# Attention's last two heads: one exponential in place of two for three packs, with rounding and two remainders on VectorE

## What is computed

```
scores = jnp.einsum('bqhd,bkhd->bhqk', q, k) / np.sqrt(HD).astype(np.float32)
mask = jnp.tril(jnp.ones((l, l), dtype=bool))
scores = jnp.where(mask, scores, jnp.float32(-1e+30))
p = jax.nn.softmax(scores, axis=-1)
o = jnp.einsum('bhqk,bkhd->bqhd', p, v)
```

## Time and profile before

| | us |
|---|---|
| median of three runs | 2253.05 (2245.42 to 2260.81) |
| the profiled execution, its time | 2254.39 |
| the profiled execution, its span | 2252.3 |
| attention's remainders on GpSimd, first to last start | 346.1 to 686.4 |
| drain, from the last head's row maxima to the next stage's first matmul | 663 to 690.8 |

### The profile page before, as it was taken

The page is one execution under the profiler, slowest core; times in us unless marked ns, Lnnn a source line. Parts: engine busy times, 40 slices in busy tenths (PEclk is TensorE's granted clock), DMA queues, the critical chain, the costliest instruction groups (busy, mean ns, idle before and its releaser), DMA issues.

```text
span 2252.3 us, 34615 instructions
## 1 busy us (share of the span) xinstructions
PE 2123.3 (94%) x11176; PEld 1724.2 (77%) x11176; DVE 1452.6 (64%) x1950; ACT 1087.4 (48%) x1700; POOL 1180.6 (52%) x717
## 2 busy tenths in 40 slices
PE   6898989999997999799999999999889999999999
PEld 4777766666666888688888899999667877877877
DVE  6787766777765888445655537776856565756563
ACT  3444447888884877622222336666523232223231
POOL 0111137999997887400000068777667376665463
PEclk8999988999998999899999999999999999999999
DMA  5678763333324765377898657878988699797795
GB/s 187 206 237 259 249 184 86 96 105 98 99 68 135 274 228 215 131 237 260 302 324 272 217 195 281 303 299 303 323 292 279 219 321 327 252 298 253 253 320 194
DMA packets 259627, 516.92 MB, mean 230 GB/s; under 512 B 20978, under 2 KB 136690, under 8 KB 240964
## 3 DMA queue, kind: packets, MB, share of 16 engines
q1 hardware_dynamic: 259524, 515.60, 69.0%
HBM read 359.81 MB, written 155.45 MB: 229 GB/s over the span
## 4 chain that ended last, share of the span: by engine, by line
PE 69%; DVE 10%; DMA 8%; issue 5%; ACT 5%; POOL 2%; SPq 1%; DVEq 0%; ACTq 0%; POOLq 0%
PE s_m_psG L2341 8%; PE s_m_psU L2341 8%; PE s_psF L2925 7%; PE s_psF L2926 7%; PE s_psF L2927 7%; PE s_w_psA L1907 5%; PE s_w_psB L1907 5%; PE s_psO L922 4%; DMA s_q_xc<-xP 4%; PE s_psS L868 4%; PE s_psX L899 3%; DVE s_a_mx L948 1%; DMA s_f_xs<-xnT 1%; PE s_w_psT L1939 1%; PE s_w_psR L1406 1%
## 5 line engine op out<-in xcount | busy, mean ns | idle before, releaser
L1053 POOL TENSOR_TENSOR s_a_pl<-s_a_pf,s_a_ph 128x1024 fp32r<-128x1024 f32 x128 | 302.0, 2394 | 22.2 <-ACT s_a_pf L1010 22.0
L2880 POOL TENSOR_TENSOR s_f_xs<-s_f_xl,s_f_xs 128x1024 f32<-128x1024 f32 x80 | 203.7, 2546 | 165.4 <-DMA s_f_xs<-xnT 165.4
L2077 POOL TENSOR_TENSOR s_w_yl<-s_w_y,s_w_yh 128x1024 fp32r<-128x1024 f32 x32 | 76.1, 2404 | 365.9 <-ACT s_w_yh L1987 365.9
L948 DVE TENSOR_REDUCE s_a_mx<-s_psS 128x1 f32<-128x512 f32 (+2 forms) x248 | 179.2, 754 | 98.8 <-PE s_psS L876 98.4
L2759 ACT ACTIVATE s_f_xh<-s_f_xs 128x1024 fp32r<-128x1024 f32 x80 | 84.8, 1060 | 309.9 <-POOL s_f_xs L2880 309.9
L2808 DVE TENSOR_TENSOR s_f_xl<-s_f_xs,s_f_xh 128x1024 fp32r<-128x1024 f32 x80 | 102.1, 1277 | 188.9 <-ACT s_f_xh L2759 188.9
L2925 PE MATMUL s_psF<-s_f_wh,s_f_xh 128*128 128x512 f32 x448 | 178.7, 399 | 9.7 <-DVE s_f_acc L2823 8.6
L449 POOL TENSOR_TENSOR s_q_qk<-s_q_ra,s_q_rb 128x1024 f32<-128x1024 f32 x16 | 37.7, 2359 | 276.6 <-DVE s_q_rb L692 276.6
L2926 PE MATMUL s_psF<-s_f_wl,s_f_xh 128*128 128x512 f32 x448 | 177.8, 397 | 0.0
L2927 PE MATMUL s_psF<-s_f_wh,s_f_xl 128*128 128x512 f32 x448 | 177.6, 396 | 0.0
L1007 ACT ACTIVATE s_a_ph<-s_psX 128x1024 fp32r<-128x1024 f32 (+1 forms) x160 | 150.6, 941 | 53.7 <-PE s_psX L904 50.0
(11 more groups left out here) (335 smaller groups left out, 6351.3 us busy)
## 6 DMA issues: line engine op xcount, KB each, us to landing
s_f_xl<-xnT SPq DMA_DIRECT2D x112, 512.0 KB, 5.3
s_f_xs<-xnT SPq DMA_DIRECT2D x80, 512.0 KB, 6.8
s_q_xt<-xT SPq DMA_DIRECT2D x16, 1024.0 KB, 7.7
s_q_xc<-xP SPq DMA_DIRECT2D x16, 1024.0 KB, 9.7
hsD<-s_q_hs SPq DMA_DIRECT2D x16, 1024.0 KB, 4.9
s_w_hin<-hsD SPq DMA_DIRECT2D x16, 1024.0 KB, 4.9
hs<-s_w_res SPq DMA_DIRECT2D x16, 1024.0 KB, 3.9
s_m_raw<-giT SPq DMA_DIRECT2D x32, 512.0 KB, 5.8
```

The costliest lines, as they stand in the source:

```text
L948: dve.tensor_reduce(mx[:, slot % 2, qi:qi + 1], psS[:, off:off + (qi + 1) * P], AX, ALU.max).then_inc(mx_ok, 1)
L1053: pool.tensor_tensor(pl[:, r, cols], pf[:, j - 1], ph[:, r, cols], ALU.subtract).then_inc(pl_ok, 1)
L2880: pool.tensor_tensor(xs[i % 3][:], xl[u % 4][:].bitcast(F32), xs[i % 3][:], ALU.add if product(u)[1][1][2] > 0 else ALU.subtract).then_inc ...
```

## The change

For heads 30 and 31 (`DRAIN`), packs 2, 3 and 4: ScalarE computes the exponential once, in full, into `pf` (one instruction in place of two, counting 2 in its semaphore). VectorE rounds it with a copy into `ph` (`high_part`, semaphore `hv_ok`). VectorE also makes the remainders of packs 2 and 4 (`low_part`, semaphore `pv_ok`); GpSimd keeps packs 1 and 3 and waits for `hv_ok` at pack 3. VectorE's new instructions stand in the step of the head's exponentials, five instructions ordered high 2, low 2, high 3, (evacuate), high 4, low 4. The waits for a remainder, on TensorE and ScalarE, go through `wait_remainder`, which picks the semaphore. Pack 0 and 1, and heads 0 to 29, are as before.

```diff
+        hv_ok, pv_ok = sem("hv_ok"), sem("pv_ok")
...
         LAST = 4
+        DRAIN = (30, 31)
+
+        def drained(head):
+
+            return head.reg is None and head.off in DRAIN
+
+        def wait_remainder(eng, head, j):
+
+            if drained(head) and j % 2 == 0:
+                eng.wait_ge(pv_ok, 2 * DRAIN.index(head.off) + j // 2)
+            elif drained(head):
+                eng.wait_ge(pl_ok, (PK - 1) * DRAIN[0] + 2 * DRAIN.index(head.off) + j // 2 + 1)
+            else:
+                eng.wait_ge(pl_ok, count(head, PK - 1, j))
+
...
             def values(s, r, g):
...
                     if half == 0:
-                        pe.wait_ge(pl_ok, count(s - 3, PK - 1, ki + 1))
+                        wait_remainder(pe, s - 3, ki + 1)
...
+            def high_part(head, j):
+
+                cols = slice(base[packs[j][0]], base[packs[j][0]] + wide[j])
+                dve.wait_ge(exp_ok, count(head, 2 * PK, 2 * j + 2))
+                dve.tensor_copy(ph[:, head.off % 2, cols], pf[:, j - 1]).then_inc(hv_ok, 1)
+
+            def low_part(head, j):
+
+                cols = slice(base[packs[j][0]], base[packs[j][0]] + wide[j])
+                dve.wait_ge(hv_ok, 3 * DRAIN.index(head.off) + j - 1)
+                dve.tensor_tensor(pl[:, head.off % 2, cols], pf[:, j - 1], ph[:, head.off % 2, cols], ALU.subtract)\
+                   .then_inc(pv_ok, 1)
...
                 if live(2):
                     remainder(s, slot)
+                    if drained(s - 2):
+                        high_part(s - 2, 2)
+                        low_part(s - 2, 2)
+                        high_part(s - 2, 3)
                 if live(0) and not (s.reg is None and s.off == 0):
                     maxima(dve, s, slot, 2)
                     maxima(dve, s, slot, 3)
                 if live(3):
                     evacuate(s - 3, (slot - 3) % 2, 0)
+                if live(2) and drained(s - 2):
+                    high_part(s - 2, 4)
+                    low_part(s - 2, 4)
...
             def exps(s, slot, j):
...
                 if j and (s - 3).exists():
-                    act.wait_ge(pl_ok, count(s - 3, PK - 1, j))
+                    wait_remainder(act, s - 3, j)
                 full = pf[:, j - 1, 0:wide[j]] if j else src
                 scale = float(1 / np.sqrt(np.float32(HD)))
+                if drained(s - 2) and j >= 2:
+                    act.activation(full, src, ACT.Exp, scale=scale).then_inc(exp_ok, 2)
+                    return
...
         def gpsimd(pool):
...
-                for j in range(1, PK):
+                for j in (1, 3) if drained(s - 2) else range(1, PK):
                     if j == 1 and (s - 4).exists():
                         pool.wait_ge(av_mm, count(s - 4, 2, 2))
+                    if drained(s - 2) and j == 3:
+                        pool.wait_ge(hv_ok, 3 * DRAIN.index(s.off - 2) + 2)
                     pool.wait_ge(exp_ok, count(s - 2, 2 * PK, 2 * j + 2))
```

## The result

The changed kernel takes 2264.86 us (median of 20 runs), the kernel before 2254.73 (20 runs): a ratio of 1.0047, 95% interval 1.0031 to 1.0064, so 7 to 14 us slower. The forecast was 2262 us, a loss of 8.5, with a range of 2250 to 2271.

What follows compares the result with a forecast made beforehand. GpSimd's remainders were taken to bound the end of attention. The locked walk added 8.5 us to the 2252.3 us span, giving 2260.8, time 2262.9, or 2261.6 from the median; forecast 2262 us, range 2250 to 2271.

Steps and rivals of the forecast that it cites:

- the lock: VectorE's copies and two-SBUF-operand remainders run one after the other with GpSimd's remainders; waiting up to 2.36 us.
- D: Drain: the locked walk plus TensorE's clock falling to 1.2 GHz after waits; +10 to +11.5 us, 2265, chance 0.20.
- the locked walk: Heads 30 and 31, main case: copies and remainders all locked against GpSimd; +8.5 us, 2262, chance 0.50.
- Steps 1 and 2: Head 30's first copy ends 672.3, remainder 673.6, second copy 674.2; head 29's first evacuation 674.8, a loss of 1.2 us.
- Step 3: GpSimd's (30,3) goes before high 4; head 29's second evacuation at 679.1 instead of 672.2, TensorE losing 4.3 us.
- Steps 4 and 7: Exponentials (31,1) begin at 680.8 instead of 676.53; TensorE finishes head 31 at 697.0 instead of 690.9, losing 6.2 us.
- Steps 5 and 6: Head 31's VectorE work waits for GpSimd; the reciprocal ends at 692.8, 11.9 us later, head 30's second evacuation at 693.4.
- Step 8: SyncE's load of the inverse lands last, at 699.4; the next stage starts then instead of 690.88, +8.5 us.
- A: Drain: only VectorE's remainders are locked, copies run beside GpSimd; +5.5 us, 2258.5, chance 0.15.
- B: Drain: no lock between VectorE and GpSimd, only queueing; the inverse lands at 692.6, +1.8 us, 2255, chance 0.08.
- C: Drain: GpSimd's queue is the only bound, VectorE's ten instructions fit its idle time; -4 us, 2249, chance 0.05.
- the 9.4 us: Four remainders taken off GpSimd at the end of attention, 2.36 us each, all counted as on the path.

Runs made afterwards that it cites:

- a8: The changed kernel with GpSimd's remainders of packs 1 and 3, heads 30 and 31, replaced by zero fills of 1024 columns; drain 25.3 us.
- a7: The changed kernel without GpSimd's remainders of packs 1 and 3, heads 30 and 31, one column of zeros written instead; drain 24.2 us.
- a6: The changed kernel with 46 spare matmuls on TensorE where it waits for the evacuations; drain 31.0 us.
- a3: The changed kernel with pack 4's rounding and remainder behind the next step's evacuation and the reciprocal one step earlier; drain 25.7 us, ratio to before 1.0018.
- a9: The changed kernel with VectorE's remainders of packs 2 and 4 taken from PSUM, no rounding on VectorE, later remainders, earlier reciprocal; drain 20.3 us, ratio to before 1.0001.
- a2: The changed kernel with pack 4's rounding and remainder moved behind the next step's evacuation of the second half; drain 26.5 us.

## Why the prediction was right, step by step

The mechanism was right: the lock, the evacuations behind VectorE's new work, and the late reciprocal. The case that happened, however, is not the one that I gave 0.50 but D, the locked walk together with a lower clock, which had 0.20 and 2265 us; the main case was 2 us short in the drain. That 2262 lies so near the measured 2264.86 is in part luck, as the interval of the loss reaches from 7 to 14 us.

**Steps 1 and 2 held to 0.1 us.** Forecast ends, with the 2.84 taken off, were 669.5 for the first copy, 670.8 for the first remainder, 671.4 for the second copy and 672.0 for the first evacuation; measured 669.48, 670.74, 671.35, 671.94. The two prices that the trace did not show held too: 0.69 for a copy, from a narrower and a wider one, and 0.55 for a blocked copy behind GpSimd's end. The Trainium skill's sentence on copies in a 2-port mode ("SBUF — State Buffer", section "Who interferes with whom") agrees with these runs: 2.76 us beside GpSimd's remainder, 1.29 beside its fill (a8) and 0.69 without either (a7).

**Step 3 came out right in an order that I had wrong.** I let GpSimd take the memory for (30,3) ahead of high 4. In fact GpSimd's instruction is listed from 671.42, VectorE's copy started 0.44 us later and still went first; GpSimd ended 3.34 after its start. The pair takes as long either way, so the second evacuation ended at 676.44 against 676.3 forecast.

**Steps 4 and 7 lacked the clock.** Exponential (31,1) was to begin at 678.0 and began at 679.49 (a6 gives 1.2 of these 1.5 back), and head 31's last groups took 6.2 instead of 3.7 us, 4.8 in the repeat. This is what rival D describes, and it happened along with the locked walk: its chance of 0.20 was too low, for the waits of 3 us that I wrote down in steps 3 and 6 were longer than the idle time of the earlier trace rows after which the clock had fallen. a6 gives its price, 1.4 to 1.6 us of the drain; D had said 1.5 to 3.

**Steps 5 and 6**, the second half, repeat steps 1 to 3 behind the late exponential: the reciprocal ended at 691.73 against 690.0 forecast. Of the 1.8 between them 1.2 are the clock's: in a6, with the clock at 1.00, it ended 24.6 us into the drain instead of 25.8.

**Step 8 named the last wait right for one execution of two.** The inverse was to land at 699.4 - 2.8 = 696.6, and TensorE to be through with head 31 at 694.2. They came at 698.06 and 698.5: the inverse 1.5 late, the values 4.3 late, 1.8 by the late reciprocal and 2.5 by the slow matmuls. So the last wait there was the values' by 0.4 us; in the repeat it was the inverse, as forecast, and TensorE stood 1.14 us for it. Either way the drain is 10.3 to 10.5 us longer, 2 more than the 8.5 of the sum, most of it the clock's. The 10.1 between the medians (2264.86 - 2254.73) agrees with it, within an interval of 7 to 14. The rest of the kernel shifted whole: from `spread_sums` to the end 1561.5 us before and 1562.7 after.

**The rivals.** A (copies free) falls with the first copy's 2.76 us. B (no lock) priced the pure queueing at +1.8; a7, where nothing is locked, shows +2.1. That they come so close may be chance: B counts GpSimd's remainders and a clock that stays high, and a7 has no remainders on GpSimd and a low clock at its end. C (faster) rested on GpSimd's queue being the only bound and VectorE's idle time being free. It fails even with the order put right: a3 does all of the new work and is still 3.6 us over the kernel before. And the 9.4 us that the prediction called "all of it on the path" were not worth that much: a9 takes the same four remainders off GpSimd, stretches nothing, and gains 1.7. There TensorE waits for its PSUM banks instead (3.6 us in three waits).

## What to carry to other kernels

Moving work to an idle engine is priced by what stands behind it in that engine's queue, not by the engine's idle share: 4.5 us of new work for each head delayed two 0.69 us evacuations and a reciprocal, and the same work a few lines further down cost 6.0 us less. VectorE does not relieve GpSimd when both read and write SBUF; give it the operand that is in PSUM (a9: 1.22 us beside GpSimd), or count the two as one engine. And where two waits end together, take both away before judging either, and read more than one execution before saying which is the last.

## What the runs showed of the hardware

A copy of 1024 float32 columns on VectorE from SBUF to SBUF waits for a GpSimd instruction that only writes (1.29, 1.00 and 1.04 us instead of 0.69, in a8), and ends 0.55 us after it. A start in the trace is not always the moment from which GpSimd keeps VectorE out: a remainder listed 0.44 us ahead of VectorE's copy was still passed by it (0.68 us for the copy, 3.34 instead of 2.39 for GpSimd), in both heads and in both executions of the changed kernel, while a fill listed 0.46 us ahead was not (a8: the fill took its 0.95 us, the copy 1.04). Whether the kind of instruction makes the difference is open. So is a smaller one in a2: GpSimd's remainder at 672.74 took 2.76 us instead of 2.36, beside two evacuations, though VectorE's next copy was listed only 1.04 us later and ended 0.55 after it. Two-input instructions on VectorE with one operand in PSUM ran at 1.22 us beside GpSimd's in a9.

TensorE's granted clock was 0.55 over 691 to 699 us behind a wait of 4.1 us, 0.72 over the same stretch behind 4.2 us in the repeat of the same program, and 1.00 over 688 to 699 us in a6, where 16 spare matmuls stood in that wait.
